# A graph and expert network on one core: maxima spread by one matmul, the last residual on GpSimd, two queue orders in the first expert stage

## The reference, cut to what matters

```python
x = x + L0_gnn(layernorm(x), src, dst, edge_weight)   # weighted segment sum and a linear map
x = x + L0_ffn(layernorm(x))                          # top-1 of 8 experts, capacity, relu 256-1024-256
x = x + L1_gnn(layernorm(x), edge_index, edge_attr)   # attention over edges and self loops, 4 heads
x = x + L1_ffn(layernorm(x))                          # top-2 of 8 experts, gelu 256-512-256

def L1_gnn(x, ...):
    e = leaky_relu(x_l[src] + x_r[dst] + ea @ W_e, 0.2)
    logits = einsum('ehc,hc->eh', e, att)
    m = segment_max(logits, dst)
    a = exp(logits - m[dst])
    alpha = a / segment_sum(a, dst)[dst]
    out = segment_sum(x_l[src] * alpha, dst)
    return elu(out + x @ W_res + bias)                # out + x @ W_res is the residual of the change
```

## Time and profile before

| what | us |
|---|---|
| median of 3 runs | 2709.13 (2708.75 to 2711.45) |
| profiled execution: time | 2709.53 |
| profiled execution: span | 2707.5 |
| first expert stage, from the first hidden layer to the last output | 870.6 to 1139.6 |
| attention loop | 1249.9 to 2298.3 |
| end of attention | 2299.6 to 2391.1 |

### The profile page before, as it was taken

How to read it: one execution, slowest core, us unless ns; L and a number is a source line. 1 busy time by engine, 2 the same in 40 slices (tenths; PEclk the granted TensorE clock), 3 DMA queues, 4 the chain that set the end, 5 groups by cost and what they waited for, 6 DMA issues and landing times. The chain is left out here.

```text
span 2707.5 us, 60532 instructions
## 1 busy us (share of the span) xinstructions
PE 2342.0 (87%) x16680; PEld 1917.4 (71%) x16680; DVE 1849.5 (68%) x6928; ACT 1473.6 (54%) x4628; POOL 1277.4 (47%) x1302
## 2 busy tenths in 40 slices
PE   5885869998885988887999999999999999437994
PEld 3774537886653655546999999999999998317993
DVE  8785799999877235275666666667666666774334
ACT  1881004444422222255888888888888888633441
POOL 1246777777762776044444444444444442004551
PEclk9996679999996989998999999999999999568997
DMA  5314334444433345133222222233232432251224
GB/s 176 104 30 111 101 95 101 104 102 103 105 97 124 105 154 173 55 127 119 73 73 71 72 71 73 73 72 73 69 74 72 132 70 38 87 189 61 72 71 160
DMA packets 252450, 259.39 MB, mean 96 GB/s; under 512 B 143396, under 2 KB 202815, under 8 KB 251876
## 3 DMA queue, kind: packets, MB, share of 16 engines
q0 software_dynamic: 57344, 151.11, 20.0%
q1 hardware_dynamic: 191476, 101.18, 13.3%
q10 hardware_dynamic: 3312, 3.28, 0.3%
HBM read 196.38 MB, written 59.06 MB: 94 GB/s over the span
## 5 line engine op out<-in xcount | busy, mean ns | idle before, releaser
L2331 POOL DMA_INDIRECT l_rows<-xl_tab,l_ra x454 | 444.0, 978 | 573.7 <-DMA l_ra<-rec_a 456.7
L2472 DVE CUSTOM_DVE_ANT_0 l_junk<-l_ps_lb,l_pen 128x256 bf16<-128x256 f32 x908 | 331.4, 421 | 282.3 <-PE l_ps_lb L2434 282.2
L1031 POOL DMA_INDIRECT room_a<-h_tab,c_rec x432 | 438.2, 1014 | 139.2 <-issue 79.0
L1078 PE MATMUL c_ps<-room_a 128*128 128x256 f32 x864 | 310.5, 449 | 84.5 <-DVE room_a L1360 45.0
L1048 ACT ACTIVATE s_cum<-iota_f,c_row_f 128x128 f32<-128x128 f32 x391 | 122.8, 389 | 311.3 <-PE c_ps_s L1116 204.9
L1078 PEld LDWEIGHTS c_ps<-room_a 128*128 128x128 f32 x864 | 161.4, 211 | 183.2 <-DVE room_a L1360 125.7
L2404 PE MATMUL l_ps_ag<-l_val,l_hot 128*128 128x260 f32 x908 | 256.4, 405 | 0.1
L2369 ACT ACTIVATE l_val<-l_rows,l_val 128x64 f32<-128x64 f32 x908 | 241.7, 337 | 7.4
L2359 ACT ACTIVATE room_a<-room_a,l_cexp x908 | 241.2, 345 | 1.1 <-issue 1.0
L2394 PE MATMUL l_bank_l<-g_att_d,l_rz 128*128 128x4 f32 x1816 | 241.3, 253 | 0.3 <-ACT l_rz L2381 0.3
L2434 PE MATMUL l_ps_lb<-ident,l_ls 128*128 128x128 f32 x1816 | 235.7, 273 | 0.0
(11 more groups left out here) (607 smaller groups left out, 5463.7 us busy)
## 6 DMA issues: line engine op xcount, KB each, us to landing
m_w<-in_L_ffn_w SPq DMA_DIRECT2D x16, 1024.0 KB, 8.2
rec_a<-room_a SPq DMA_DIRECT2D x114, 102.0 KB
l_ra<-rec_a SPq DMA_DIRECT2D x227, 51.0 KB, 2.1
e_w<-in_L_ffn_W SPq DMA_DIRECT2D x16, 512.0 KB, 12.4
l_rows<-xl_tab,l_ra POOLq DMA_INDIRECT x454
room_a<-h_tab,c_rec POOLq DMA_INDIRECT x432, 2.8
xrr_tab<-q_xrr SPq DMA_DIRECT2D x25, 256.0 KB, 2.0
e_w<-ye_buf SPq DMA_DIRECT2D x4, 1280.0 KB, 9.3
```

The lines of the kernel that those rows point to most:

```text
L1031: pool.indirect_dma_start(rows[:, u, :], None, K["h_tab"], bass.IndirectOffsetOnAxis(ap=rec[:, n % RSLOTS, k, 0:1].bitcast(I32), axis=0)). ...
L1078: pe.matmul(ps[s % NB][:, :], hot[:, u, :], rows[:, s % RU, :], start=True, stop=True).then_inc(s_agg, 1)
L2331: pool.indirect_dma_start(rows[:, u, j, :], None, K["xl_tab"], bass.IndirectOffsetOnAxis(ap=ra[:, u, j, A_SRC:A_SRC + 1].bitcast(I32), axi ...
L2472: dve.tensor_tensor_reduce(junk[:, h, :], ps_lb[:, h, :], pen[:, v3, :], 1.0, -3.0e38, ALU.add, ALU.max, tmax[:, v3, h:h + 1]).then_inc(S[ ...
```

## The change

Four edits. In the attention, the three pieces of the maximum now lie side by side in one tile `pieces` (all f32), one 12-column matmul for each half spreads them into 12 columns of PSUM, and DVE adds the three with a new `tensor_reduce` into `mdst`, placed between the second and the third of the four maxima; `arg` then subtracts `mdst`. In the first expert stage, `gather(n + 2)` is issued ahead of the scatters of part n instead of behind them, and the wide block moves from SP's step 4 to its step 5. At the end of attention, POOL adds the residual to the own term for chunks 0 to 3, five instructions of one tile each, and DVE waits for it (`s_res`) before the one addition left in C; chunk 4 is as before.

```diff
-                if s == 4:
+                if s == 5:
                     sp.wait_ge(s_staged, PARTS_A)
...
             for n in range(PARTS_A):
+                gather(n + 2)
                 pool.wait_ge(s_staged, n + 1)
...
-                gather(n + 2)
...
-        mlow = t("mlow", [P, U, HEADS], BF16)
+        pieces = t("pieces", [P, U, 3, HEADS], F32)
+        mnew, mrest, mlow = (pieces[:, :, k, :] for k in range(3))
+        mdst = t("mdst", [P, U, SUB, HEADS], F32)
...
                     for j in range(SUB):
-                        for n, part in enumerate((mlow[:, v, :], uppers(mrest[:, v, :]), uppers(mnew[:, v, :]))):
-                            mm = pe.matmul(ps_md[v % 2][:, j, :], hot_b[:, v, j * P:(j + 1) * P], part,
-                                           start=(n == 0), stop=(n == 2))
+                        mm = pe.matmul(ps_md[v % 2][:, j, :, :].rearrange("p k h -> p (k h)"),
+                                       hot_b[:, v, j * P:(j + 1) * P],
+                                       uppers(pieces[:, v, :, :].rearrange("p k h -> p (k h)")), start=True, stop=True)
...
-                    for h in range(HEADS):
+                    for h in range(2):
                         dve.tensor_tensor_reduce(junk[:, h, :], ps_lb[:, h, :], pen[:, v3, :], 1.0, -3.0e38,
...
                     dve.wait_ge(S["md"], r4 + 1)
-                    dve.tensor_tensor(arg[:, v4, :, :], ls[:, v4, :, :], ps_md[v4 % 2], ALU.subtract).then_inc(S["arg"], 1)
+                    dve.tensor_reduce(mdst[:, v4, :, :], ps_md[v4 % 2].rearrange("p j k h -> p j h k"), AX.X, ALU.add
+                                      ).then_inc(S["ms"], 1)
...
+                    dve.wait_ge(S["ms"], r4 + 1)
+                    dve.tensor_tensor(arg[:, v4, :, :], ls[:, v4, :, :], mdst[:, v4, :, :], ALU.subtract
+                                      ).then_inc(S["arg"], 1)
...
+        @block.gpsimd
+        def _(pool):
+            for k in range(BY_POOL):
+                pool.wait_ge(s_sc, k + 1)
+                pool.wait_ge(s_in[k], 32)
+                for tile in range(k * CT, (k + 1) * CT):
+                    ins = pool.tensor_tensor(z[:, tile, :], z[:, tile, :], xrr(tile, 1)[:, 0, D:2 * D], ALU.add)
+                ins.then_inc(s_res, 1)
...
                     dve.wait_ge(s_sc, k + 1)
-                    o.did(dve.tensor_tensor(z4, acc[:, :, :, 0:HC], z4, ALU.add))
-                    o.then()
-                    dve.tensor_tensor(z[:, ts, :], z[:, ts, :], xrr(k * CT, CT)[:, :, D:2 * D], ALU.add).then_inc(s_n, 1)
+                    if k < BY_POOL:
+                        dve.wait_ge(s_res, k + 1)
+                        dve.tensor_tensor(z4, acc[:, :, :, 0:HC], z4, ALU.add).then_inc(s_n, 1)
```

More of the change, by code:

```diff
@@ L2257, in attend @@
         junk = t("junk", [P, HEADS, SUPER], BF16)
-        tmax, mnew, dm, cexp = (t(n, [P, U, HEADS], F32) for n in ("tmax", "mnew", "dm", "cexp"))
-        mrest = t("mrest", [P, U, HEADS], F32)
-        mlow = t("mlow", [P, U, HEADS], BF16)
+        tmax, dm, cexp = (t(n, [P, U, HEADS], F32) for n in ("tmax", "dm", "cexp"))
+        pieces = t("pieces", [P, U, 3, HEADS], F32)
+        mnew, mrest, mlow = (pieces[:, :, k, :] for k in range(3))
+        mdst = t("mdst", [P, U, SUB, HEADS], F32)
         AGW = HEADS * (HC + 1)
@@ L2272, in attend @@
         ps_ag = [c.enter_context(nc.psum_tensor(f"l_ps_ag{k}", [P, 512], F32)) for k in range(2)]
-        ps_md = [ps[:, AGW + AUX:AGW + AUX + SUB * HEADS].rearrange("p (j h) -> p j h", j=SUB) for ps in ps_ag]
+        ps_md = [ps[:, AGW + AUX:AGW + AUX + SUB * 3 * HEADS].rearrange("p (j k h) -> p j k h", j=SUB, k=3)
+                 for ps in ps_ag]
         s_ra = [sem(f"l_ra{k}") for k in range(U)]
         s_rows = K["dma_sems"]("l_rows", U)
-        names = ("hot stk_ps hot_c stk_c z rz lg ls lb tm mn mr ml dm mst c md arg a val1 val ag sc acc pb"
+        names = ("hot stk_ps hot_c stk_c z rz lg ls lb tm mn mr ml dm mst c md arg a val1 val ag sc acc pb ms"
                  ).split()
@@ L2475, in step @@
                     dve.wait_ge(S["md"], r4 + 1)
-                    dve.tensor_tensor(arg[:, v4, :, :], ls[:, v4, :, :], ps_md[v4 % 2], ALU.subtract).then_inc(S["arg"], 1)
+                    dve.tensor_reduce(mdst[:, v4, :, :], ps_md[v4 % 2].rearrange("p j k h -> p j h k"), AX.X, ALU.add
+                                      ).then_inc(S["ms"], 1)
+                if on3:
+                    for h in range(2, HEADS):
+                        dve.tensor_tensor_reduce(junk[:, h, :], ps_lb[:, h, :], pen[:, v3, :], 1.0, -3.0e38,
+                                                 ALU.add, ALU.max, tmax[:, v3, h:h + 1]).then_inc(S["tm"], 1)
+                if on4:
+                    dve.wait_ge(S["ms"], r4 + 1)
+                    dve.tensor_tensor(arg[:, v4, :, :], ls[:, v4, :, :], mdst[:, v4, :, :], ALU.subtract
+                                      ).then_inc(S["arg"], 1)
                 if live(s, 2, SUPERS):
@@ L2559, in attend_finish @@
             sem("f_" + n) for n in ("dve", "la", "lap", "lac", "z", "zc", "d", "e", "n", "en"))
-        s_lin, s_co, s_sc = (sem("f_" + n) for n in ("lin", "co", "sc"))
+        s_lin, s_co, s_sc, s_res = (sem("f_" + n) for n in ("lin", "co", "sc", "res"))
+        BY_POOL = NC - 1
         s_in = K["s_fin"]
@@ L2690, in _ @@
                     dve.wait_ge(s_sc, k + 1)
-                    o.did(dve.tensor_tensor(z4, acc[:, :, :, 0:HC], z4, ALU.add))
-                    o.then()
-                    dve.tensor_tensor(z[:, ts, :], z[:, ts, :], xrr(k * CT, CT)[:, :, D:2 * D], ALU.add).then_inc(s_n, 1)
+                    if k < BY_POOL:
+                        dve.wait_ge(s_res, k + 1)
+                        dve.tensor_tensor(z4, acc[:, :, :, 0:HC], z4, ALU.add).then_inc(s_n, 1)
+                    else:
+                        o.did(dve.tensor_tensor(z4, acc[:, :, :, 0:HC], z4, ALU.add))
+                        o.then()
+                        dve.tensor_tensor(z[:, ts, :], z[:, ts, :], xrr(k * CT, CT)[:, :, D:2 * D], ALU.add
+                                          ).then_inc(s_n, 1)
                 if step >= 3:
```

## The result

The changed kernel takes 2683.22 us, the median of four runs (2679.45 to 2685.26), beside 2710.29 us for the kernel before in the same measurement (2708.75 to 2711.64). The ratio is 0.9903, with a 95% interval from 0.9889 to 0.9916. The prediction was 2683.0, range 2673 to 2694.

A forecast was written before the change was run, and what follows sets the result against it. The prediction took PE's instruction stream to bound the attention, and the chain scatters, staging, cleaning, store, weights the first expert stage. -22.5 - 5.0 + 1.5 = -26.0 us on the median of 2709.1 gives 2683, range 2673 to 2694.

The forecast's parts named there:

- The maxima: Attention: two 12-column matmuls for six 4-column ones save 0.10 us in each of 227 supersteps, taken as 22.5 us.
- The price by count: Attention, PE: a 12-column matmul costs about what a 4-column one does, 25 to 27 ns.
- The slower rival: Attention: the reduction delays `arg` beyond reserves of 1.05 us; at 1.2 us delay the kernel takes 2740; chance 4%.
- The first expert stage: Expert 5's weights are in at 1041.2 and its hidden layer starts near 1041.5 instead of 1046.48: -5.0 us.
- the slip: First expert stage: four gathers now ahead of each part's scatters make scatters, staging, cleaning and store 5.1 us later.
- the slow clock: Expert 5's hidden layer after its wait: 16.66 against 13.90 us, left unchanged since some 4 us of wait remain.
- The end of attention: POOL takes over residual additions: waits +2.2, chunks 2 and 3 save 1.53 each, held instructions +2.4; +1.5 us.
- the +2.4 for held instructions: End of attention: DVE instructions with two SBUF operands stand still during POOL's additions, some 0.6 us each, +2.4 us.
- the scatters don't slip: First expert stage, rival: weights come at 1036, -12.0 us instead of -5.0, 2676 in all; chance 13%.
- they slip twice as much: First expert stage, rival: scatters slip by 10 us instead of 5, gain 0, 2688 in all; chance 10%.
- the maxima's change doesn't do what it says: Attention, rival: the six matmuls lie under L2394's weight load, leaving -3.5 us, 2706 in all; chance 8%.
- DVE stands behind all of POOL's additions: End of attention, rival: +6 us instead of +1.5, 2688 in all; chance 3%.

The follow-up runs named there:

- only_maxima: The kernel before with only the changed spreading of the maxima in the attention (`attend()` of the changed kernel): 2686.61 us, ratio 0.9913.
- spread_thrice: The changed kernel with each 12-column matmul that spreads the maxima issued three times instead of once: 2704.15 us, ratio 0.998 against the kernel before.
- five_sums: The changed kernel with DVE's sum over the spread maxima done five times, four into a spare tile: 2685.23 us, ratio 0.9905 against the kernel before.
- only_orders: The kernel before with only the two changed orders of the first expert stage, gathers ahead of scatters and wide block later: 2702.64 us, ratio 0.9973.
- only_residual: The kernel before with only the changed residual at the end of attention (`attend_finish()` of the changed kernel): 2710.17 us, ratio 1.0002.
- only_wide: The kernel before with only the wide block of weights moved behind store 3 instead of store 2: 2704.83 us, ratio 0.9977.
- only_clean_early: The kernel before with only DVE's cleanings put ahead of its stagings in the first expert stage: 2702.08 us, ratio 0.9961.
- residual_23: The changed kernel with POOL adding the residual for chunks 2 and 3 only: 2683.49 us, ratio 0.99 against the kernel before.

## Why the prediction was right, point by point

**The maxima: -22.5 forecast, -21.9 in the attention loop of every profile, 20.0 to 27.4 faster by only_maxima's ratio.** (The longer stretch to `f_ps_la` is 22.4 us shorter in only_maxima and 19.4 and 21.1 in the two profiles of the changed kernel; the spread lies ahead of the loop.) The rows stand as forecast: period 4.46 us, two matmuls in 0.06 us, no wait of PE for ACT's result beyond single cases, DVE idle 1.14 where 1.0 to 1.1 was named, since the reduction fills its other wait. The price by count held up in spread_thrice. The reduction costs 0.18 us by duration and 0.09 in DVE's stream, and five_sums shows that five of them cost the loop 1.2 us in all. The slower rival, which needed 1.05 us of delay, was far off.

**The first expert stage: -5.0 forecast; -8.3 in the profile of the changed kernel, -6.4 in the means of all nine profiles.** The mechanism is right: new waits for the cleaned buffer and for weights, store 2 later, expert 5 earlier. Two of its sizes are not. First, the slip. Store 2 went out at 1029.80 with 1029.2 forecast, but that it fits so well is luck: the first hidden layer itself came 1.8 us later in this profile. Counted from there, the store slipped by 3.8 us (from 153.5 to 157.4; 4.2 in the means of three profiles each) and not by 5.1. Expert 5's hidden layer starts 174.8 us after the first one in the mean of the three profiles with the old orders, and 170.8 in the six with the new ones: -4.0 for the -5.0 of the sum. In four of the six it no longer waits for its weights at all; its start is then set by PE's own work behind expert 4, which waited for weights itself and ran slowly behind that wait (15.41 us here, 16.8 to 17.1 in the others). Second, the slow clock, the term that I put at nothing. I left the 16.66 us of expert 5's hidden layer as they were, because I still expected a wait of some 4 us ahead of it. I had said that experts 3 and 4 would come later and had not carried that into the gap ahead of expert 5: the gap was 0 to 2 us, and the hidden layer took 13.9 to 14.0 us in all six profiles where the three with the old orders have 16.2 to 16.7, which is -2.4 us. Together -6.4.

**The end of attention: +1.5 forecast, +3.0 in the profile, of which the residual explains 0.3.** From DVE's step on the linear logits of chunk 1 to the table load, the kernel before takes 2391.64 - 2321.40 = 70.24 us and the changed one 2368.78 - 2298.24 = 70.54. These are the four instructions:

```profile
2321.40 0.17 DVE L2662 TENSOR_TENSOR f_lg<-f_lg,f_ps_lin 128x20 f32<-128x20 f32 x1 [2.94 <-PE f_ps_lin L2619]
...
2391.64 1.28 ACT L2854 ACT_TABLE_LOAD   x1 [8.75 <-PEq L2521]
```

```profile
2298.24 0.18 DVE L2683 TENSOR_TENSOR f_lg<-f_lg,f_ps_lin 128x20 f32<-128x20 f32 x1 [4.64 <-PE f_ps_lin L2640]
...
2368.78 1.28 ACT L2880 ACT_TABLE_LOAD   x1 [8.75 <-PEq L2532]
```

The same distance is 70.2 us in all six profiles with the old residual and 70.5 in five of the six profiles with POOL's additions for chunks 0 to 3 (70.9 in five_sums), whatever the clock ahead of it, so the 0.3 us are the residual's. The other 2.7 us lie ahead of it, in PE at the lower clock; the wait in brackets grew from 2.94 to 4.64. That only_orders shows the same (4.64) without touching this code is the reason to call it the clock's doing. As for the residual itself: the wait in chunk 0 came as forecast, the one in chunk 1 did not (DVE was itself held back until POOL had finished at 2322.74), and chunks 2 and 3 had none. By time chunk 1 is right all the same: its C ends 2.1 us later from that step on, 2.2 were forecast. The term that was too large is the +2.4 for held instructions. The three at 0.65 to 0.70 us in chunk 1 stand in the time in which DVE would have waited for POOL anyway, so they were counted twice. Behind chunk 1 two are clearly longer, and two more by 0.1 to 0.2 us, together 1.2 us:

```profile
2330.65 1.96 DVE L2674 SCALAR_TENSOR_TENSOR g_xr_p<-g_xr_p,g_att_l 128x1280 f32<-128x1280 f32 x1
...
2343.94 0.65 DVE L2695 TENSOR_TENSOR f_rden<-f_rden,f_ca 128x20 f32<-128x20 f32 x1
```

With these, 2.1 - 3.1 + 1.2 gives about the 0.3 measured. The page "SBUF — State Buffer" of the Trainium skill, on which the prediction drew, fits these rows; no run here separates its lock from another form of contention. The part came out 1.2 us below my +1.5, and only_residual, at 1.0002 [0.9992, 1.0013], has the change as a whole at nothing.

**The sum.** -26.0 forecast, -24.0 in the span, -26.3 by the ratio of the runs. That it fits to a few tenths is partly luck. Two terms came out better than forecast, the stage by 1.4 us and the residual by 1.2; against them stand the maxima, 0.6 us short, and the clock behind the attention, which the sum had no term for (the last two stretches are 1.9 us longer, of which the residual explains 0.3). The unchanged code ahead of these stages differs by up to 3 us between profiles by chance. Of the rivals, "the scatters don't slip" and "they slip twice as much" fell with store 2, 3.8 us later in the stage; "the maxima's change doesn't do what it says" fell with the 0.06 us, and "DVE stands behind all of POOL's additions" with chunks 2 and 3, where it waits for none.

**What stays open.** Why the clock drops earlier after the attention's last superstep in some kernels: the group with the earlier loss has kernels with and without changed maxima, orders and residual. Whether the early gathers or the wide block carry the 15 us beside DVE's new order. In five_sums the last two stretches are 93.5 and 316.1 us, 1.9 more in sum than in the changed kernel; that was not followed up.

## What to carry to other kernels

Where one engine is busy throughout, count the instructions in its stream: at 4 and at 12 columns a matmul with its weight load cost the same 25 to 27 ns, so three merged into one saved two of them. In a loop whose engines feed each other through their queues, an order on one queue has no price of its own: the early gathers cost 4 us alone and nothing beside the moved weights, and both together gained some 6 us with DVE's old order and 15 once its cleanings stood ahead of its stagings. So look for the long wait with needed work queued behind it (here DVE's 20 us at L1873) before tuning the queues around it.

## What the runs showed of the hardware

The granted clock moves 2 to 3 us between kernels that differ only elsewhere. After the attention, a stretch of unchanged code took 89.8 to 89.9 us in the kernel before and only_wide and 92.3 to 92.6 in only_orders and only_maxima; in only_orders PE stood at 0.50 in place of 0.61 for 8 us. A wait can be paid twice: behind the 9.17 us wait of the earlier trace rows came 2.8 us of slow matmuls, and only_clean_early lost nearly as much in slow matmuls behind its three waits as in the waits. It is not always so: in only_orders expert 5's hidden layer took 14.00 us behind a wait of 1.76 us. GpSimd's additions lengthened only a few of VectorE's instructions beside them: 0.65 to 0.70 us in place of 0.18, and 1.96 in place of 1.49. And an earlier start of a stage can be given back, as residual_23 shows with a clock of 0.79 where the changed kernel had 1.00.
